# A loop of two rows on five engines, written out as straight code

## The reference

```
x = x + attn(layernorm(x))      # projections, short convolution of 4 taps, silu, rotary,
                                # gated linear attention with 64 slots (two scans), gate, Wo
x = x + xattn(layernorm(x), ctx)  # 16 heads of 16 over 77 context tokens, masked softmax
x = x + ffn(layernorm(x))       # 8 experts of width 64, the best 2 per token weighted
```

## Time and profile before

| | us |
|---|---|
| median of 3 runs | 1814.25 |
| lowest, highest run | 1811.79, 1815.97 |
| span of the profiled execution | 1817.2 |
| PE busy in it | 1666.7 (92%) |
| DVE busy | 1496.2 (82%) |
| ACT busy | 889.4 (49%) |
| POOL busy | 774.7 (43%) |
| instructions | 36129 |

### The profile page before, as it was taken

One profiled execution on the slowest core, in us unless ns is written; L12 is line 12 of the kernel. 1 busy time (PEld: TensorE's weight loads), 2 busy tenths in 40 slices (PEclk: granted clock), 3 DMA queues, 4 the chain that ended last, 5 costly groups with the idle time before them and its releaser, 6 DMA issues.

```text
span 1817.2 us, 36129 instructions
## 1 busy us (share of the span) xinstructions
PE 1666.7 (92%) x12064; PEld 1497.1 (82%) x12064; DVE 1496.2 (82%) x3540; ACT 889.4 (49%) x2351; POOL 774.7 (43%) x809
## 2 busy tenths in 40 slices
PE   3699999999999999999999999999999999999986
PEld 3588888889888888888888988888888888898875
DVE  4778888888888888888888888888888888888652
ACT  2255544455554455555445555444555444555441
POOL 2344444444544444444444454444444444445320
PEclk9899999999999999999999999999999999999887
DMA  4000000000000000000000000000000000000000
GB/s 113 9 9 1 15 15 15 14 14 0 14 14 14 14 14 14 0 14 14 14 14 14 12 2 14 14 14 14 14 0 14 14 14 14 14 10 5 9 7 12
DMA packets 44572, 24.99 MB, mean 14 GB/s; under 512 B 24432, under 2 KB 44528, under 8 KB 44528
## 3 DMA queue, kind: packets, MB, share of 16 engines
q1 hardware_dynamic: 44528, 24.43, 5.1%
HBM read 16.03 MB, written 8.39 MB: 13 GB/s over the span
## 4 chain that ended last, share of the span: by engine, by line
PE 56%; DVE 30%; issue 9%; ACT 4%; DVEq 0%; DMA 0%; SPq 0%; POOL 0%; ACTq 0%; POOLq 0%
PE bank L377 49%; DVE a_conv L809 6%; PE bank L611 4%; DVE x_nmax L942 3%; DVE dve_scrap L252 2%; DVE a_xn L759 2%; PE bank L383 2%; DVE f_xn L759 2%; ACT x_prob L1211 2%; DVE a_E L792 1%; DVE a_stats L746 1%; DVE x_stats L746 1%; DVE f_s L1018 1%; DVE f_th L1013 1%; DVE x_xnT_lo L774 1%
## 5 line engine op out<-in xcount | busy, mean ns | idle before, releaser
L1211 ACT ACTIVATE x_prob<-bank,x_nmax 128x77 f32<-128x77 f32 x1024 | 247.7, 327 | 167.9 <-DVE x_nmax L942 163.7
L377 PEld LDWEIGHTS bank<-x_Vx,x_probT 77*128 77x128 f32 x2048 | 251.6, 193 | 2.9
L377 PE MATMUL bank<-x_Vx,x_probT 77*128 77x17 f32 x2048 | 246.2, 255 | 0.0
L1222 ACT ACTIVATE x_probT<-bank 77x512 f32<-77x512 f32 x256 | 152.4, 595 | 92.0 <-PE bank L611 92.0
L942 DVE TENSOR_REDUCE x_nmax<-bank 128x4 f32<-128x308 f32 x256 | 121.3, 474 | 59.8 <-PE bank L377 58.4
L611 PE MATMUL bank<-ident,x_prob 128*77 128x128 f32 x1024 | 155.9, 275 | 0.4 <-ACT x_probT L1222 0.4
L809 DVE SCALAR_TENSOR_TENSOR a_conv<-a_raw,cw,a_conv 128x256 f32<-128x256 f32 x384 | 156.2, 477 | 0.0
L1306 POOL TENSOR_TENSOR x_rstd<-x_ve,mhalf 128x2 f32<-128x2 f32 x32 | 22.6, 706 | 301.2 <-DVE x_ve L752 301.2
L1330 POOL TENSOR_TENSOR a_Er_lo<-a_E,a_Er_hi 128x512 fp32r<-128x512 f32 x32 | 74.2, 2320 | 142.2 <-ACT a_Er_hi L1114 142.2
L611 PEld LDWEIGHTS bank<-ident,x_prob 128*77 128x77 f32 x1024 | 124.0, 148 | 7.6 <-issue 0.6
L377 PE MATMUL bank<-x_K_bd,x_Q_stack 128*128 128x308 f32 x256 | 98.6, 385 | 15.0 <-ACT x_prob L1211 12.3
(11 more groups left out here) (250 smaller groups left out, 5585.2 us busy)
## 6 DMA issues: line engine op xcount, KB each, us to landing
x<-in_x SPq DMA_DIRECT2D x32, 256.0 KB, 2.9
out<-x SPq DMA_DIRECT2D x32, 256.0 KB, 2.2
ctxT<-in_ctxT SPq DMA_DIRECT2D x32, 77.0 KB, 2.5
keep<-in_mask SPq DMA_DIRECT2D x32, 19.2 KB, 2.6
f_s<-in_fWu SPq DMA_DIRECT2D x2, 256.0 KB, 5.6
a_AT<-in_Wv SPq DMA_DIRECT2D x1, 256.0 KB, 3.8
a_okn<-in_Ws SPq DMA_DIRECT2D x1, 256.0 KB, 3.9
a_qn<-in_Wg SPq DMA_DIRECT2D x1, 256.0 KB, 3.8
```

Of the source, the lines that this page charges most:

```text
L377: return pe.matmul(out, lhsT, rhs, start=start, stop=stop, skip_group_check=True)
L1211: ins = act.activation(prob[:, u % 2, i, :], X0[:, i * S2:(i + 1) * S2], ACT.Exp, scale=-1.0, bias=nmax[:, u % 2, i:i + 1])
L1222: act.activation(probT[:, u % 2].rearrange("p h t -> p (h t)"), X1[0:S2, :], ACT.Copy).then_inc(on.x_pT, 1)
```

## The change

The `Fori` of the four compute engines and that of SP become Python loops over the same values. `half` is then a number at build time, so 26 bodies stand in the program where two stood, each wait has a constant, and each DMA a constant address. Nothing else is touched: the steps, their order, the buffers and the semaphores with their values are the same. The loop's body holds, for two rows, 24 register operations and 12 separate waits or loop instructions on PE, 42 and 15 on DVE, 25 and 10 on ACT, 7 and 6 on POOL, 2 and 7 on SP; besides them every engine has a branch into the loop and one back. In the changed kernel's bodies there are none of these.

```diff
--- before.py
+++ after.py
@@ -261,7 +261,7 @@
             body(Row(1, 1), Row(1, 0), Row(0, 1), Row(0, 0))
             body(Row(2, 0), Row(1, 1), Row(1, 0), Row(0, 1))
             last = B // 2
-            with eng.Fori(2, last - 1) as half:
+            for half in range(2, last - 1):
                 body(Row(half, 1), Row(half, 0), Row(half - 1, 1), Row(half - 1, 0))
                 body(Row(half + 1, 0), Row(half, 1), Row(half, 0), Row(half - 1, 1))
             body(Row(last - 1, 1), Row(last - 1, 0), Row(last - 2, 1), Row(last - 2, 0))
@@ -355,7 +355,7 @@
             body(Row(0, 1), Row(0, 0), None)
             body(Row(1, 0), Row(0, 1), Row(0, 0))
             body(Row(1, 1), Row(1, 0), Row(0, 1))
-            with sp.Fori(2, B // 2 - 1) as half:
+            for half in range(2, B // 2 - 1):
                 body(Row(half, 0), Row(half - 1, 1), Row(half - 1, 0))
                 body(Row(half, 1), Row(half, 0), Row(half - 1, 1))
             last = B // 2
```

## The result

The changed kernel took 1822.22 us (median of 4 runs, 1816.51 to 1823.51), the kernel before 1815.11 us (4 runs, 1811.79 to 1816.48): ratio 1.0039, 95% interval 1.0021 to 1.0058, slower by 7.1 us where 4.2 us faster was forecast. The kernel before kept to medians of 1815.1 to 1815.9. The profiled execution of the changed kernel is the fastest of its four: 1816.51 us with a span of 1814.7, so some 1.8 us lie around the span.

What follows compares the result with a forecast made beforehand. The bound was a chain alternating between TensorE (56%) and VectorE (30%). The median 1814.25 us less 4.17 us of loop cost, with zero for addresses and fetch and falls unchanged, gave 1810.1 us; range 1806.8 to 1814.2.

Steps and rivals of the forecast that it cites:

- Steps 1 and 2: Loop branches, counters, register operations and register waits go on all engines: gain 4.17 us, bounds 4.0 and 4.3.
- Step 3: DMA addresses on SP become constants: zero, as no compute engine waits for a load or store after the start.
- Step 4: Instruction fetch added by the longer program, at most 78 packets of 16 KB and 52 of 8 KB: taken as zero.
- Step 5: Falls of PE's clock, 1.40 us each, are not touched by the change; their number can differ by chance.
- The rival with "one or two more" falls: One or two more clock falls in the median run: 1811.5 or 1812.9 us; chance 0.24.
- The rule weighed: A taken branch to a target outside two 16 KiB pages waits for a fetch; PE's loop trace was said to disagree.
- The rival on the slower side: Instruction blocks queue behind each row's 256 KB load and store, 1.1 us per row: 1838.7 us; chance 0.06.

Runs made afterwards that it cites:

- e2: The changed kernel plus eight overwritten matmuls per row where PE waits, ahead of the stretch of the clock's falls; 1805.50 us, ratio 0.9943.
- e5: The kernel before, loop kept, with three overwritten matmuls of 512 columns added per row where PE waits; 1812.69 us, ratio 0.9986.
- e6: The kernel before with only the loop of the four compute engines written out, SP keeping its own; 1822.93 us, ratio 1.0046.
- e9: The changed kernel less one VectorE filler instruction per row on the chain, for a shorter body; 1822.79 us, ratio 1.0056.
- e10: The changed kernel with both the filling of e2 and the left-out instruction of e9; 1803.93 us, ratio 0.9943.
- e7: The kernel before with the compute engines' loop holding four rows, six passes, two rows written out behind; 1835.32 and 1836.15 us, ratio 1.0114.
- e3: The kernel before, loop kept, with the same eight overwritten matmuls per row as e2; 1838.11 us over 12 runs.
- e1: The changed kernel run again without any edit; 1818.17 us over 12 runs, ratio 1.0015.
- e8: The changed kernel plus five overwritten matmuls per row at another place, ahead of the transposes of v; 1817.13 us, ratio 1.0012.
- e4: The changed kernel plus one VectorE instruction of 128x96 elements per row on the chain, for a longer body; 1817.92 us, ratio 1.0007.

## Why the prediction was wrong, by its steps

- *Steps 1 and 2, branch and register operations: right.* Forecast 4.17 us for the 26 bodies; the first profile has 20 bodies of 53.29 us and gives 4.37 once the falls are taken off, and the pair of e2 and e5, both without falls, gives 4.56.
- *Step 3, SP's addresses: right*, e6.
- *Step 4, fetch at zero: right* for this program (98 and 70 packets, no plain body of another length in either profile of it). In e9 and e10 one body each came 0.36 us late without a semaphore, and in e6 one came 0.18 us late; that may be a block of instructions that arrived late (in e10 one of 8 KB comes at 1360.92, behind the gap that ends at 1360.26), and wasn't tried.
- *Step 5 failed:* "Their number can differ from run to run by chance of position." The sum took over the three falls of before and added nothing for more. But the number of falls is no chance laid over the body's length, it depends on it. At 54.69 us a body with a fall comes back to nearly the same place for the next one. The rival with "one or two more" falls (chance 0.24) had the right direction, as a matter of chance and not of length, and too small a size: the two profiles have six and nine falls where the profile of before had three. At 1.40 us each, three to six more falls cost 4.2 to 8.4 us. That takes the 4.2 gained and gives back up to as much. The medians of the three straight builds lie 2.5 to 7.1 us above the kernel before; for 7.1 us with the gain of 4.2 it takes an estimated eight more falls in the median run than in that of before, and no trace of such a run was kept.
- What was there to be read: the fall's price (1.40) and the straight body (53.29) give 54.69. The distance at which falls repeat could not be read there, since the three falls of before lie 215 us and more apart; but their place in the body could have been laid beside the body's length. The earlier trace rows shows the same 1.89 us of PE ahead of a fall and ahead of none; I took that as "not seen" instead of asking which lengths of a body bring one fall after another.
- *A slip in the sum:* it set the profile's span of before (1817.2) beside times of runs and found it 2.9 us above the median. A run's time is some 1.8 us longer than its span, so on that scale the profile was some 4.7 us above the median. The forecast doesn't depend on it.
- *The rule weighed:* the trace of before made me doubt the rule of the Trainium skill on branches (Runtime: NRT & Kernel Launch, Instruction fetch mechanics). Its consequence didn't show there, since the loop was kept whole without a fetch; e7 and e3 show it at work, at 3.5 to 5.6 us of standing still per back edge where it happens. The window of two 16 KiB pages that the section names doesn't fit: the loop of before, six packets of 16 KB by the earlier trace rows, was kept.
- The rival on the slower side (fetch meets data, once a row) is not what happened, and the range, which ended at no gain, left out the true case.

## What to carry to other kernels

A saving of 0.16 us per row in a long, even pipeline can move its period into step with something that it doesn't control, here the falls of TensorE's clock. Look at the clock of each body before trusting a change of 0.2%, and compare runs by the number of bodies that fell. If PE idles at one place per iteration and the clock falls behind it, a few matmuls with no use put right there (1.0 us of them per row here) can be worth more than the code that is saved. In straight code they gained 12.7 us (e2 against e1), in the looped kernel 3.3 (e5); the straight code by itself lost 2.5 to 7.1, and both together gained 10. And before a loop is lengthened, count PE's instructions in it: 32 more in two rows were enough for waits of up to 5.6 us at back edges, and 12 more were not.

## What the runs showed of the hardware that was not expected

- Falls of the clock follow each other at 54.6 us, one per body, when a body with a fall takes 54.61 to 54.70 us; with 54.83 to 54.85 us they came singly (three of three), and in the kernel before (54.77 to 54.91) too.
- The fall comes behind a stretch with PE busy 1.9 of 3.4 us and not behind one with 2.9 at the same place, though bodies with 1.9 and no fall stand beside it; e8 shows that work some 6 us ahead of that stretch doesn't help.
- PE held a loop of two rows with three added matmuls per row without any fetch, and with eight added it waited at some back edges and not at others (five out of twelve in the profile). Where the limit lies, whether it is the number alone or also where the loop begins among the fetched blocks, and why only some edges miss, stays open.
- Rows of two to five begin at different places in different runs, but not anywhere. In each of the four profiles with two rows (the changed kernel, e1, e6, e8) the second begins 481.3 us behind the last fall of the first, and the single falls of e4 are 535.9 us apart, twice. So the place in the body decides where a row begins, too. What sets the first row's place in a run, and why the first profile has no third row where its time would have come (1429.2 us), stays open.
